# Turning the quantised weights by DMA transposes from ACT's queue instead of by TensorE

## The reference

```
def lpbq_dequant(w):                       # blocks of 32 along the input axis
    s = maximum(max(abs(wb), axis=-1) / 7, 1e-12)
    return clip(round(wb / s), -8, 7) * s
def act_qdq(x):                            # one step for the whole tensor
    scale = maximum(max(abs(x)) / 32767, 1e-12)
    return clip(round(x / scale), -32768, 32767) * scale

h    = act_qdq(einsum('bsd,bdh->bsh', x, W[cat]) + b[cat][:, None, :])
up   = act_qdq(h @ lpbq_dequant(w_up).T)
gate = act_qdq(h @ lpbq_dequant(w_gate).T)
gate = act_qdq(gate * fixed_qdq_u16(sigmoid(gate)))
out  = x + act_qdq(gate * up) @ lpbq_dequant(w_down).T
```

## Time and profile before

| | us |
|---|---|
| median of 3 runs | 990.96 |
| lowest and highest | 990.79 and 992.87 |
| the profiled execution | 992.62 |
| its span, first to last instruction | 990.8 |
| TensorE busy | 901.8 |
| VectorE busy | 654.7 |
| ScalarE busy | 445.9 |
| mean granted clock of TensorE | 0.962 of full |

### The profile page before, as it was taken

One profiled execution on the slowest core, in us unless ns is written; L12 is line 12 of the kernel. 1 busy time (PEld: TensorE's weight loads), 2 busy tenths in 40 slices (PEclk: granted clock), 3 DMA queues, 4 the chain that ended last, 5 costly groups with the idle time before them and its releaser, 6 DMA issues.

```text
span 990.8 us, 13547 instructions
## 1 busy us (share of the span) xinstructions
PE 901.8 (91%) x4904; PEld 487.8 (49%) x4904; DVE 654.7 (66%) x755; ACT 445.9 (45%) x469; POOL 4.0 (0%) x17
## 2 busy tenths in 40 slices
PE   6999998999999999999999999990029999999998
PEld 5999994444444444444444444440014444444443
DVE  0365778756656654469788789758987787876511
ACT  1112341433333333398787782228875444544000
POOL 0000000000000000000000000000000000000000
PEclk9999998999999999999999999995559999999999
DMA  8998864323352222579999635999987799988221
GB/s 282 376 385 298 292 217 173 125 98 127 127 222 96 97 95 95 218 268 419 374 380 388 241 127 195 390 423 362 417 333 268 275 348 344 345 304 319 85 85 64
DMA packets 67768, 249.67 MB, mean 252 GB/s; under 512 B 5971, under 2 KB 5971, under 8 KB 67731
## 3 DMA queue, kind: packets, MB, share of 16 engines
q1 hardware_dynamic: 58354, 198.72, 54.5%
q10 hardware_dynamic: 9376, 50.48, 12.6%
HBM read 175.51 MB, written 73.66 MB: 251 GB/s over the span
## 4 chain that ended last, share of the span: by engine, by line
PE 86%; DMA 5%; DVE 4%; ACT 2%; issue 2%; DVEq 0%; POOL 0%; SPq 0%; ACTq 0%; POOLq 0%
PE bank L705 16%; PE bank L706 16%; PE bank L707 16%; PE bank L655 11%; PE bank L740 6%; PE bank L741 6%; PE bank L742 6%; DMA up_ring<-up_scratch 3%; ACT umag L607 2%; PE wt_bank L666 2%; PE bank L643 1%; DMA x_ring<-in_x_dram 1%; PE bias_bank L741 1%; PE wt_bank L740 1%; PE wt_bank L741 1%
## 5 line engine op out<-in xcount | busy, mean ns | idle before, releaser
L527 ACT ACTIVATE stage<-bank 128x512 f32<-128x512 f32 x192 | 112.9, 593 | 228.6 <-PE bank L707 218.0
L934 DVE TENSOR_REDUCE tile_max<-stage 128x1 f32<-128x1536 f32 (+1 forms) x62 | 108.4, 1749 | 41.9 <-ACT stage L527 41.9
L740 PE MATMUL bank<-wt_down,o_even 128*128 128x512 f16 x192 | 73.8, 384 | 66.7 <-DVE o_even L1142 66.7
L705 PE MATMUL bank<-xq_head,wt_gate 128*128 (+1 forms) x336 | 128.3, 382 | 4.3 <-DVE xq_head L921 4.3
L706 PE MATMUL bank<-xq_head,wt_gate 128*128 (+1 forms) x336 | 128.4, 382 | 0.0
L707 PE MATMUL bank<-xq_head,wt_gate 128*128 (+1 forms) x336 | 128.2, 382 | 0.0
L705 PE MATMUL bank<-xq_head,wt_up 128*128 x336 | 127.3, 379 | 0.0
L706 PE MATMUL bank<-xq_head,wt_up 128*128 x336 | 127.3, 379 | 0.0
L707 PE MATMUL bank<-xq_head,wt_up 128*128 x336 | 127.3, 379 | 0.0
L655 PE MATMUL bank<-xt,w_ring 128*128 128x128 f32 x1024 | 121.6, 278 | 2.2 <-ACT xt L480 2.2
L655 PEld LDWEIGHTS bank<-xt,w_ring 128*128 128x128 f32 x1024 | 118.9, 195 | 2.4 <-ACT xt L480 2.4
(11 more groups left out here) (156 smaller groups left out, 1361.6 us busy)
## 6 DMA issues: line engine op xcount, KB each, us to landing
up_ring<-up_scratch SPq DMA_DIRECT2D x60, 768.0 KB, 7.0
w_ring<-in_L_cond_W_dram SPq DMA_DIRECT2D x32, 1024.0 KB, 7.2
gate_scratch<-stage ACTq DMA_DIRECT2D x32, 768.0 KB, 3.3
gate_ring<-gate_scratch SPq DMA_DIRECT2D x32, 768.0 KB, 7.9
up_scratch<-stage ACTq DMA_DIRECT2D x32, 768.0 KB, 7.0
product_scratch<-prod_ring SPq DMA_DIRECT2D x19, 768.0 KB, 6.4
back_ring<-product_scratch SPq DMA_DIRECT2D x19, 768.0 KB, 13.1
gate_even<-gate_scratch SPq DMA_DIRECT2D x16, 768.0 KB, 7.4
```

The costliest lines, as they stand in the source:

```text
L527: nc.scalar.activation(stage[:, q % 2, n % PIECE_TILES, :], psum[n % BANKS][:, :], ACT.Copy)\
L705: nc.tensor.matmul(bank[:, :], w_hi, x_hi, start=(k == 0), stop=False)
L740: nc.tensor.matmul(bank, o_hi, wt_down[:, 0, k, :], start=(k == 0), stop=False)
L934: V.tensor_reduce(tile_max[:, side, bass.ds(Q * i + q, 1)], stage[:, q % 2, :, :].rearrange("p t c -> p (t c)"), AX.X, ALU.max, apply_abso ...
```

## The change

PE no longer turns weights, and ACT no longer copies them out of PSUM. Instead ACT issues, once both parts of a slice are there, two DMAs with `transpose=True`, one per part, each reading 128x512 f16 from `wparts` and writing four 128x128 blocks to the same places as before. It stands where `copy_wt` stood. A slot of `wparts` is free again when both its DMAs have landed, counted by one semaphore per slot (`wt_ready[j]`, 32 per slice). PE waits for all gate slices before the gate pass, for all up slices before the up pass, for all down slices before the down stage. ACT waits for all before the first gate code, whose successors overwrite `wparts`. ACT's loops over conditioning chunks 5 to 7 and gate chunks 1 to 3 and 5 to 7 are written out, chunk by chunk; PE's become one loop each.

```diff
-        w_high, w_low, w_turned, wt_ready = sem("w_high"), sem("w_low"), sem("w_turned"), sem("wt_ready")
+        w_high, w_low = sem("w_high"), sem("w_low")
+        wt_ready = [sem(f"wt_ready{n}") for n in range(SLICES)]
...
 def high_part(w, it, j, first):
                 if not first:
-                    act.wait_ge(w_turned, n - SLICES + 1)
+                    act.wait_ge(wt_ready[j], 32 * (KH * w + it))
...
-            def copy_wt(w, it, j):
+            def turn_wt(w, it, j):
                 n = WSLICES * w + SLICES * it + j
-                act.wait_ge(w_turned, n + 1)
-                if w < 2:
-                    dst = (wt_gate, wt_up)[w][:, :, :, bass.ds((SLICES * it + j) * P, P)]
-                else:
-                    dst = wt_down[:, :, 4 * j:4 * j + 4, bass.ds(it * P, P)]
-                nc.scalar.activation(dst, wt_bank[:, :, :, :], ACT.Copy).then_inc(wt_ready, 1)
+                act.wait_ge(w_low, n + 1)
+                for h in range(2):
+                    if w < 2:
+                        dst = (wt_gate, wt_up)[w][:, h, :, bass.ds((SLICES * it + j) * P, P)]
+                    else:
+                        dst = wt_down[:, h, 4 * j:4 * j + 4, bass.ds(it * P, P)]
+                    act.dma_start(dst, wparts[:, j, h, :], transpose=True).then_inc(wt_ready[j], 16)
...
-            with act.Fori(5, CHUNKS) as i:
+            for i in range(5, CHUNKS):
                 cond_chunk(i, False, True)
-            copy_wt(0, KH - 1, SLICES - 1)
+            turn_wt(0, KH - 1, SLICES - 1)
...
                         if j == 0:
+                            for w_slot in range(SLICES):
+                                act.wait_ge(wt_ready[w_slot], 96 * KH)
                             gate_code(0)
...
-            def turn_w(w, it, j, first):
-                n = WSLICES * w + SLICES * it + j
-                pe.wait_ge(w_low, n + 1)
-                if not first:
-                    pe.wait_ge(wt_ready, n)
-                for h in range(2):
-                    for k in range(4):
-                        mm = nc.tensor.transpose(wt_bank[:, h, k, :], wparts[:, j, h, k * P:(k + 1) * P], ident16[:, :])
-                mm.then_inc(w_turned, 1)
...
                     cond_matmul(i, r, first)
-                    if weights and r >= 1:
-                        turn_w(0, i - 4, r - 1, isinstance(i, int) and i == 4 and r == 1)
...
                     tile_matmul(i, i, n, wt_gate, first)
-                    if late and n >= NT - SLICES:
-                        turn_w(w, it, n - NT + SLICES, False)
-                    if not late and n % 4 == 3:
-                        turn_w(w, it, n // 4, False)
...
-            pe.wait_ge(wt_ready, WSLICES)
+            for j in range(SLICES):
+                pe.wait_ge(wt_ready[j], 32 * KH)
+            gate_chunk(0)
+            with pe.Fori(1, CHUNKS - 1) as i:
+                gate_chunk(i)
+            gate_chunk(CHUNKS - 1)
+            for j in range(SLICES):
+                pe.wait_ge(wt_ready[j], 64 * KH)
...
+            for j in range(SLICES):
+                pe.wait_ge(wt_ready[j], 96 * KH)
             pe.wait_ge(tile_copied, 2 * NT * CHUNKS)
```

More of the change, by code:

```diff
@@ L503, in cond_chunk @@
                     if weights and r == 0 and not first_slice:
-                        copy_wt(0, i - 5, SLICES - 1)
+                        turn_wt(0, i - 5, SLICES - 1)
                     if weights and r >= 1:
@@ L507, in cond_chunk @@
                     if weights and r >= 2:
-                        copy_wt(0, i - 4, r - 2)
+                        turn_wt(0, i - 4, r - 2)
             cond_chunk(0, True, False)
@@ L544, in gate_chunk @@
                         if n >= NT - SLICES:
-                            copy_wt(w, it, n - NT + SLICES)
+                            turn_wt(w, it, n - NT + SLICES)
                     else:
@@ L549, in gate_chunk @@
                         if n % 4 == 3:
-                            copy_wt(w, it, n // 4)
+                            turn_wt(w, it, n // 4)
             gate_chunk(0, True, 1, True)
-            with act.Fori(1, 4) as i:
+            for i in range(1, 4):
                 gate_chunk(i, False, 1, False)
             gate_chunk(4, False, 2, True)
-            with act.Fori(5, CHUNKS) as i:
+            for i in range(5, CHUNKS):
                 gate_chunk(i, False, 2, False)
@@ L657, in cond_matmul, with cond_chunk @@
                 mm.then_inc(cond_done, 1)
-            def turn_w(w, it, j, first):
-                n = WSLICES * w + SLICES * it + j
-                pe.wait_ge(w_low, n + 1)
-                if not first:
-                    pe.wait_ge(wt_ready, n)
-                for h in range(2):
-                    for k in range(4):
-                        mm = nc.tensor.transpose(wt_bank[:, h, k, :], wparts[:, j, h, k * P:(k + 1) * P], ident16[:, :])
-                mm.then_inc(w_turned, 1)
-            def cond_chunk(i, first, last, weights):
+            def cond_chunk(i, first, last):
                 for r in range(BPC):
@@ L685, in _ @@
             mm.then_inc(bias_summed, 1)
[L686 to L692, removed]
+            cond_chunk(0, True, False)
+            with pe.Fori(1, CHUNKS - 1) as i:
+                cond_chunk(i, False, False)
+            cond_chunk(CHUNKS - 1, False, True)
             def tile_matmul(i, c, n, wt, first):
@@ L708, in tile_matmul, with gate_chunk @@
                 mm.then_inc(tile_done, 1)
-            def gate_chunk(i, w, late):
-                it = i if w == 1 else i - 4
+            def gate_chunk(i):
                 first = isinstance(i, int) and i == 0
```

## The result

| | us |
|---|---|
| before, median of 6 runs | 992.53 |
| after, median of 6 runs (984.25 to 988.09) | 987.34 |
| ratio after to before | 0.9946, 95% interval 0.9929 to 0.9963 |
| profiled execution after, and its span | 987.43 and 985.6 |

A forecast was written before the change was run, and what follows sets the result against it. TensorE, busy 91% of the span, was taken to bound the kernel. Removing 18.0 us and adding 1.5 gave -16.5, from 991.0 to 974.5 us; own range 972 to 980, 8-in-10 range 972 to 1001.

The forecast's parts named there:

- Removed from TensorE, 18.0 us: Conditioning and gate pass: 35 weight turns of 0.45 us off the path, 15.8 us, plus 2.2 us of waits.
- Issue, 1.3 us: ACT's queue: each transposing DMA takes 1.3 us to issue; six per conditioning chunk, 7.8 us, stay hidden.
- the limit of 1.9: Conditioning chunks: each of six issues may take 1.9 us before ACT sets the pace.
- Added to the DMA engines: 72 transposes of 128 KB; in conditioning, if they cost as much as plain bytes, they just fit beside the loads.
- the 370 of the row: 370 GB/s, the average the queues moved from 13 to 81 us, with TensorE at the same batch pace.
- Landing, 5 us and hidden: wparts slots: transposes land in 5 us, plain transfers in 3.3 to 7.5; slot needed again after 12 us, so hidden.
- Start of the gate pass, 1.5 us late: First gate matmul waits for all 24 gate transposes beside the w_up load: -1.1 to +5.0 us late, taken as 1.5.
- rival 2: Chunks 4 to 7: slow landings make wparts slots set the pace; 7.5 us a pair adds 26 us, 1000.5; chance 0.20.
- rival 1: Conditioning: issues fill ACT's queue, deciding from 1.9 us each; at 2.6, 17 us lost, 991; range 976 to 1010; chance 0.17.
- The far end: Rival 2's extreme: 1309 ns per block, 31.4 us a chunk, kernel about 1036 us; 0.05 of that rival's chance.
- Rival 3: Conditioning gains nothing because TensorE waits for w_ring; only the gate pass gains 13.0 us, giving 979.5; chance 0.08.

## Why the prediction was wrong, point by point

**Removed from TensorE, 18.0 us: right.** The gate pass fell by 13.1 (forecast 24 x 0.45 + 2.2 = 13.0), and where both causes of loss are out, the total falls by 18 to 19.

**Issue, 1.3 us: right in size.** The median is 1.30 to 1.33, by the one row that I took as the upper bound. What the step left out is that an issue can be blocked: up to 5.1 us here, over the limit of 1.9. With half of the matrix bytes the longest took 2.2.

**Added to the DMA engines, "just fit": borne out.** On SP's queue the same transposes and the full matrix loads went through while TensorE kept its pace (17.00 of 17.00 and 18.00 of 18.00 us). In the changed kernel, too, TensorE never waited for w_ring. So the bytes fitted, though their sum (327 and 49 GB/s) stood a little over the 370 of the row; but such a sum says nothing of when a single transfer lands.

**Landing, 5 us and hidden: the step that failed.** The prediction argued that ACT's queue has no megabytes ahead of the pair, and so took 5 us with 7.5 as the upper bound, against 12 us until the slot is needed again. It measured 10.4 us by the median in conditioning and up to 15.7: beside the matrix loads the transposes landed one after another, the first six 3.7 us apart. So neither the slots nor ACT's issues stayed hidden: 11.9 us of waits for landed pairs, 15.3 at the issues, and 10.7 of TensorE for xt. The runs show the reverse of the argument on queues: 10.4 us from ACT's, 6.0 from SP's, behind the very megabytes. In the gate pass, at 2.5 to 3.4 us, the landing was below what I took, and it costs nothing there.

**Start of the gate pass, 1.5 us late: mis-sized.** The wait became 7.8 us where 4.7 are for codes, so 3.1 us late, within the -1.1 to +5.0 given. The place was right, and the w_up load was the right suspect.

**The ledger.** Forecast of the gate pass's start: 3.5 us earlier. Measured: 8.8 later. Of the 12.3 between, 1.6 are the late start over what I had taken, and the rest is conditioning: the last matmul there begins at 156.7 where it was 151.0, in place of 5.0 earlier. The rows of the conditioning matmuls, before and after:

```profile
L655 PE MATMUL bank<-xt,w_ring x1024: 274/275/422, 13.5 to 151.0; 128*128 128x128 f32 x171
```

```profile
L659 PE MATMUL bank<-xt,w_ring x1024: 274/275/421, 13.5 to 156.7; 128*128 128x128 f32 x171
```

8.5 of those 10.7 are waits for xt that were not there before. Of the rest, 0.8 has nothing to do with the transposes: the batch that started at 82.6 before starts at 83.5 after, and the first transpose is issued at 90.8. From 91.6 us on, the batch starts lie 9.9 us further apart in sum than undisturbed ones, so the last 1.4 are lost around the same waits.

**The rivals.** What happened is rival 2's mechanism, at a smaller price than the 26 us I gave it, and with rival 1's symptom: both showed in the trace as the text said (high parts and the first gate matmul waiting for a DMA into wt_gate, landings over 6 us; ACT's queue full of issues, TensorE waiting for xt). I had treated them as two causes with a limit each; they are one backlog with two outlets, as the run with nine slots shows. The 7.5 us a pair that I took for it was nearly right at first (7.3 us), but the twelve pairs went from 90.8 us, the first issue, to 164.6, the last landing: 73.8 us, 6.2 a pair, since the landings come quickly once the loads have ended. Rival 2's own sum with 6.2 in place of 7.5 adds 10 us and not 26. The outcome thus lay between the ends to which the text gave its chances; that it still fell inside the wide range 972 to 1001, which was made to reach over the rivals, is no success of the forecast. The far end, 1309 ns for each block by the Trainium skill's page VectorE: DVE Perf Modes (the three transpose paths), was of no use: a DMA of four blocks lands in 2.5 us, where four one after another would take 5.2 (an estimate from that page's figure). Rival 3 did not occur.

**The rule on bandwidth.** The Trainium skill's page DMA: Bandwidth & Descriptors (latency and other measured facts) gives 261 GB/s for a transposing DMA with a non-contiguous middle dimension. On SP's queue the trace agrees: from 143.0 to 145.0 us five transposes landed 0.5 us apart, 128 KB each, which is 262 GB/s (an estimate from the landings). On ACT's queue beside the matrix loads, 128 KB every 3.7 us is 36 GB/s, so the figure says nothing of a queue that shares the engines. The same page (queues, rings and completion order) says that an engine goes round between queues packet by packet. If its packets are those that the profile counts, a stream of small packets waits for a large one of the other queue at every turn. The three landings (6.4, 8.5 and 10.4 us) and the two queues (3.7 and 0.5 us apart) go in that direction; but by the counts of the queue row a copy in pieces has 528 packets and a transpose 544, nearly the same, and they differ by 2 us. So it is not the whole, and the packets themselves were not looked at. That part stays argued.

## What to carry to other kernels

Moving work from the bounding engine to DMAs pays where the engines are idle (the gate pass: 13.1 us, with the engines' share at 0.54 from 200 to 233 us) and not beside a stream of large loads; change one stage at a time, for here the good two thirds of the change hid behind the bad one. Of a new DMA ask not only whether its bytes fit, but on whose queue it stands and what else that engine must do while the queue is blocked: the same transposes made the gate pass start 8.8 us later from ACT's queue, and 4.7 us earlier from SP's, with the loads of x moved up and that of w_up behind them. And a wait for everything ahead of a stage can be split into waits for what each tile needs.

## What the runs showed of the hardware

- A transposing DMA of 128x512 f16 takes 1.2 to 1.3 us of the issuing sequencer on either queue, against 0.34 for a plain store, 0.57 for a plain copy of the same 128 KB in rows and 0.66 in pieces (medians).
- An issue on a queue that is behind can stand still: up to 5.1 us, with four earlier transposes not yet landed (though another issue with as many under way took 1.3). Plain copies in 256-byte pieces did it too (up to 3.4 us), transposes on SP's queue up to 3.0, rows of 1 KB hardly (0.93).
- Landings beside the matrix loads, medians from the start of the issue: 6.4 us for rows of 1 KB, 8.5 for pieces of 256 bytes, 10.4 for the transpose, all on the other queue, and 6.0 for the transpose on the loads' own queue. The first six transposes landed 3.7 us apart on the other queue, and those of a pair 0.4 to 0.6 us apart on the loads' own.
- The table's share of the DMA engines went to 1.18 in a stage that kept its pace, so over 1 it is no measure of what is left.
